# Two cross-attentions in one kernel: four exponential buffers, the keys ahead of the value products' sum, and a unit's normalisation at the end of ScalarE's and GpSimd's order

## The reference, cut to what is computed

```
x = x + tanh(g_xattn[0]) * xattn0(layernorm(x), ctx)      # 8 heads of 64
x = x + tanh(g_ffn[0])   * expert_choice(layernorm(x))    # sinkhorn, 16 experts
x = x + tanh(g_xattn[1]) * xattn1(layernorm(x), ctx)      # 16 heads of 64
x = x + tanh(g_ffn[1])   * top2_experts(layernorm(x))     # 8 experts

def xattn(x, context, Wq, Wk, Wv, Wo, bo):
    q, k, v = heads(x @ Wq), heads(context @ Wk), heads(context @ Wv)
    attn = softmax(q k^T * 64**-0.5)
    return merge(attn v) @ Wo + bo
```

## Time and profile before

| | |
|---|---|
| time, three runs | 2080.51, 2082.16, 2084.51 us; median 2082.16 |
| profiled execution | 2078.9 us, its span 2077.2 us |
| PE busy | 1849.3 us, 89% of the span |
| DVE, ACT, POOL busy | 77%, 76%, 31% |
| first attention | from about 30 to 383 us |
| second attention | from about 1360 to 1950 us |
| granted TensorE clock, mean | 0.973 |
| DMA transposes (L534) | 192, 3.0 us to landing |

### The profile page before, as it was taken

One profiled execution on the slowest core, in us unless ns is written; L12 is line 12 of the kernel. 1 busy time (PEld: TensorE's weight loads), 2 busy tenths in 40 slices (PEclk: granted clock), 3 DMA queues, 4 the chain that ended last, 5 costly groups with the idle time before them and its releaser, 6 DMA issues. The chain is left out here.

```text
span 2077.2 us, 73737 instructions
## 1 busy us (share of the span) xinstructions
PE 1849.3 (89%) x29130; PEld 1340.8 (65%) x29130; DVE 1599.2 (77%) x3619; ACT 1578.8 (76%) x2771; POOL 652.4 (31%) x893
## 2 busy tenths in 40 slices
PE   4898888784899999999999999968888889999698
PEld 3677777642466666666666667745666667777487
DVE  3778777797788888888888887767888887777654
ACT  3777778473798989898989898747777778887543
POOL 3677777502000000000000000035555555455465
PEclk9999999897799999999999999979999999999899
DMA  7433334275000000000000000046555553333233
GB/s 176 96 83 82 84 84 87 70 270 208 11 12 14 14 14 12 14 12 14 12 14 12 14 9 2 2 116 137 128 128 128 128 128 64 63 60 61 53 108 116
DMA packets 304575, 147.44 MB, mean 71 GB/s; under 512 B 235472, under 2 KB 289536, under 8 KB 304000
## 3 DMA queue, kind: packets, MB, share of 16 engines
q1 hardware_dynamic: 303824, 144.75, 28.1%
q10 hardware_dynamic: 560, 0.08, 0.0%
HBM read 55.45 MB, written 30.54 MB: 41 GB/s over the span
## 5 line engine op out<-in xcount | busy, mean ns | idle before, releaser
L1640 DVE TENSOR_TENSOR h<-g,h 128x1024 f16<-128x1024 f32 x256 | 313.3, 1224 | 140.9 <-ACT h L1585 140.9
L232 PEld LDWEIGHTS psE<-ew,h 128*128 128x128 f16 x6144 | 349.9, 98 | 54.6 <-issue 35.6
L232 PE MATMUL psE<-ew,h 128*128 128x128 f16 x6144 | 363.7, 219 | 11.9 <-DVE eo L1650 5.2
L232 PE MATMUL psH<-xg,ew 128*128 128x512 f16 x1536 | 356.1, 382 | 0.0
L1580 ACT ACTIVATE g<-psH,eb1T 128x512 f32<-128x512 f32 x512 | 330.4, 680 | 29.5 <-PE psH L232 23.0
L580 PE MATMUL psV<-Bw,cT 96*64 96x512 f16 x2304 | 319.7, 380 | 31.1 <-DVE vB L786 31.1
L755 POOL TENSOR_TENSOR E<-E,rden 128x512 f32<-128x512 f32 x192 | 200.1, 1042 | 257.0 <-DVE rden L795 257.0
L1585 ACT ACTIVATE h<-g 128x1024 f16<-128x1024 f32 x256 | 270.6, 1057 | 8.1
L1708 POOL MEMSET rbias<- 64x384 f32 x1 | 0.4, 411 | 855.6 <-POOLq L133 855.6
L660 PE MATMUL psS<-u,xTa 128*64 128x256 f32 x1536 | 209.2, 391 | 59.8 <-ACT u L718 54.5
L746 POOL TENSOR_TENSOR Ph<-E,Ph 128x512 f16<-128x512 f32 x192 | 222.4, 1159 | 120.8 <-ACT Ph L703 120.8
(11 more groups left out here) (256 smaller groups left out, 2774.3 us busy)
## 6 DMA issues: line engine op xcount, KB each, us to landing
keys_ahead<-ust SPq DMA_DIRECT2D x40, 512.0 KB, 4.8
u<-keys_ahead SPq DMA_DIRECT2D x40, 512.0 KB, 3.5
rawe<-in_L_ffn_w_dram SPq DMA_DIRECT2D x32, 256.0 KB, 2.8
wb<-rw SPq DMA_DIRECT2D x64, 128.0 KB, 2.0
rows<-places SPq DMA_DIRECT2D x110, 64.0 KB, 2.6
out_dram<-x SPq DMA_DIRECT2D x7, 512.0 KB, 3.2
context_T<-cT SPq DMA_DIRECT2D x64, 48.0 KB, 2.3
PT<-Ph SPq DMA_TRANSPOSE x192, 3.0
```

The costliest lines, as they stand in the source:

```text
L232: last = e.matmul(to, a, b, start=start and n == 0, stop=stop and n == 2, **flags)
L1640: e.tensor_tensor(h[:, 1 - par, 1, 2 * q:2 * q + 2, :], g32[:, 2 * q:2 * q + 2, :], h[:, 1 - par, 0, 2 * q:2 * q + 2, :], ALU.subtract)\
```

## The change

The exponential tile E gets four buffers in place of two, indexed by j mod 4, and the subtraction of j waits for the remainder of j-4. On PE the keys of j are issued right behind value product b (and the tokens' transpose), and PV of j-4 behind the keys. On ACT the copy Ph of j-2 goes from the middle to behind u of j; in the first attention xTa is thereby directly behind vB a. On POOL the multiply of j-1 and behind it the Ph remainder of j-2 go to the end, behind the bias and the expert weights. Nothing is added or left out.

```diff
-            E = sb(c, "E", [P, 2, 8, N], F32)
+            E = sb(c, "E", [P, 4, 8, N], F32)
...
+                    self.four = self.j.mod(4)
...
                         if a3.on:
                             values(a3, 1, "b")
+                        if first:
+                            tokens()
+                        if a.on:
...
+                            if not a.loaded:
+                                keys(a, 0)
+                                keys(a, 1)
                         if a4.on:
                             wait(e, s[f"pt{a4.par}"], ring_of(a4.j, 2, a4.par), 16)
...
                             last.then_inc(s["PV"], 1)
-                        if first:
-                            tokens()
-                        if a.on:
...
-                            if not a.loaded:
-                                keys(a, 0)
-                                keys(a, 1)
                         if a2.on:
                             values(a2, 0, "a", ready)
...
-                        if not first:
-                            tokens()
-                        if a2.on:
-                            wait(e, s["mul"], a2.j)
-                            wait(e, s[f"pt{a2.par}"], ring_of(a2.j, 2, a2.par) - 1, 16)
-                            e.activation(Ph[:, a2.par, 0].rearrange("p k t -> p (k t)"),
-                                         E[:, a2.par].rearrange("p h l -> p (h l)"), ACT.Copy)\
-                             .then_inc(s["phi"], 1)
-                        if first:
-                            tokens()
+                        tokens()
                         if a3.on:
                             value_hi(a3, 1, "b")
...
                                              psU[:, b, :], ACT.Copy).then_inc(s[f"uc{b}"], 1)
+                        if a2.on:
+                            wait(e, s["mul"], a2.j)
+                            wait(e, s[f"pt{a2.par}"], ring_of(a2.j, 2, a2.par) - 1, 16)
+                            e.activation(Ph[:, a2.par, 0].rearrange("p k t -> p (k t)"),
+                                         E[:, a2.four].rearrange("p h l -> p (h l)"), ACT.Copy)\
+                             .then_inc(s["phi"], 1)
...
+                        if a1.on:
+                            wait(e, s["rden"], a1.j)
+                            e.tensor_tensor(E[:, a1.four], E[:, a1.four],
+                                            rden[:, a1.par, :].unsqueeze(2).broadcast_to([P, 8, N]), ALU.mult)\
+                             .then_inc(s["mul"], 1)
+                        if a2.on:
+                            wait(e, s["phi"], a2.j)
+                            e.tensor_tensor(Ph[:, a2.par, 1].rearrange("p k t -> p (k t)"),
+                                            E[:, a2.four].rearrange("p h l -> p (h l)"),
+                                            Ph[:, a2.par, 0].rearrange("p k t -> p (k t)"), ALU.subtract)\
+                             .then_inc(s["plo"], 1)
...
-                            wait(e, s["plo"], a.j - 2)
-                            e.tensor_tensor(E[:, a.par], psS[:], top[:].unsqueeze(2).broadcast_to([P, 8, N]),
+                            wait(e, s["plo"], a.j - 4)
+                            e.tensor_tensor(E[:, a.four], psS[:], top[:].unsqueeze(2).broadcast_to([P, 8, N]),
```

More of the change, by code:

```diff
@@ L614, in body @@
                             values(a3, 1, "b")
+                        if first:
+                            tokens()
+                        if a.on:
+                            if a.opens:
+                                if first:
+                                    wait(e, s["ct"], a.t)
+                                else:
+                                    wait(e, s[f"ctx{a.ring}"], ring(a.t, a.ring), 16)
+                            if not a.loaded:
+                                keys(a, 0)
+                                keys(a, 1)
                         if a4.on:
@@ L628, in body @@
                             last.then_inc(s["PV"], 1)
-                        if first:
-                            tokens()
-                        if a.on:
-                            if a.opens:
-                                if first:
-                                    wait(e, s["ct"], a.t)
-                                else:
-                                    wait(e, s[f"ctx{a.ring}"], ring(a.t, a.ring), 16)
-                            if not a.loaded:
-                                keys(a, 0)
-                                keys(a, 1)
                         if a2.on:
@@ L711, in body @@
                             wait(e, s["sub"], a1.j)
-                            e.activation(E[:, a1.par], E[:, a1.par], ACT.Exp, bias=zero_col[:], scale=DH ** -0.5)\
+                            e.activation(E[:, a1.four], E[:, a1.four], ACT.Exp, bias=zero_col[:], scale=DH ** -0.5)\
                              .then_inc(s["exp"], 1)
@@ L743, in body @@
                              .then_inc(s["clo"], 1)
-                        if a2.on:
-                            wait(e, s["phi"], a2.j)
-                            e.tensor_tensor(Ph[:, a2.par, 1].rearrange("p k t -> p (k t)"),
-                                            E[:, a2.par].rearrange("p h l -> p (h l)"),
-                                            Ph[:, a2.par, 0].rearrange("p k t -> p (k t)"), ALU.subtract)\
-                             .then_inc(s["plo"], 1)
                         if a.opens:
@@ L752, in body @@
                             e.tensor_tensor(tile_of(a.t, x), tile_of(a.t, x), bo_rep[:], ALU.add).then_inc(s["bo"], 1)
-                        if a1.on:
-                            wait(e, s["rden"], a1.j)
-                            e.tensor_tensor(E[:, a1.par], E[:, a1.par],
-                                            rden[:, a1.par, :].unsqueeze(2).broadcast_to([P, 8, N]), ALU.mult)\
-                             .then_inc(s["mul"], 1)
                         if first and a.on:
@@ L792, in body @@
                             wait(e, s["mul"], a1.j - 2)
-                            e.tensor_reduce(den[:, a1.par, :], E[:, a1.par], AX.X, ALU.add).then_inc(s["den"], 1)
+                            e.tensor_reduce(den[:, a1.par, :], E[:, a1.four], AX.X, ALU.add).then_inc(s["den"], 1)
                             wait(e, s["den"], a1.j)
```

## The result

| | before | changed |
|---|---|---|
| median (9 runs each) | 2082.59 us | 2077.4 us (2070.53 to 2079.36) |
| ratio, 95% interval | 1 | 0.9966 [0.9954, 0.9979] |
| profiled execution, span | 2078.9, 2077.2 | 2073.0, 2071.3 |

A forecast was written before the change was run, and what follows sets the result against it. Taken as bound by where PE waits, in loops closing once per unit. Terms 0 (first attention), -8.4 (keys every unit), -13.2 (keys ahead), +1 (ends) sum to -20.6: 2058.3 from the profiled 2078.9, 2061.5 as median; range 2051 to 2075.

The forecast's parts named there:

- Keys every unit: Second attention, keys made each unit: a loop of 4.55 us per unit, pairs from 9.45 to 9.10, 8.4 us gained.
- Keys ahead: Second attention, odd units' keys ready made: pairs from 8.60 to 8.27 us, 40 pairs gaining 13.2 us (8 to 16).
- First attention: 60 units: PE's 0.54 us wait exchanged for another, 311.0 against 310.6 us; booked as nothing, range -3 to +12.
- The loop through L811: First attention: PV, DVE's addition (L813 before), den, vB remainder, value product, tokens, keys close a loop of 4.95 us.
- runs at PE's pace: Rival, first attention: if a counted step of the loop overlaps, 60 units gain 0.54 each; -32, time 2029; chance 0.05.
- Units 5 to 15: Second attention, five of the pairs with keys ahead: forecast to gain 1.6 us.
- Part 2: Normalisation at GpSimd's end: late remainder delays SP's keys load, odd scores 0.9 us late; pair 8.27, 13.2 us gained.
- a miss of some tenths: Second attention, keys ahead: transpose lands at 9.7 to 10.3, read at about 9.8; lateness falls into the keys' wait.
- The ends: End of each attention: last remainder follows a multiply and another remainder, 0.5 us later, twice, +1 us.
- the keys' load would push the pair beyond the old 8.60: Rival, keys ahead: load landing at L = 14.0 makes pairs 9.28, time about 2102; chance 0.06.
- DVE would be held by GpSimd in the normalisations: Rival, first attention: 18 stages each held 1.0 us by a GpSimd remainder; +18, time 2079.5; chance 0.04.

The follow-up runs named there:

- e4: The changed kernel with GpSimd's Ph remainder ahead of the bias and the multiply again in the second attention; 2067.46 us, ratio 0.9922.
- e10: The changed kernel with SP issuing the load of the ready made keys ahead of the odd unit's DMA transpose; 2069.65 us, ratio 0.9935.
- e1: The changed kernel with PV back ahead of the tokens' transpose and the keys, in the first attention alone; 2071.14 us, ratio 0.9942.
- e2: The changed kernel with DVE's addition of psY to x moved behind the next step's vB remainder in the first attention; 2040.17 us, ratio 0.9780.
- e9: The kernel before with DVE's addition of psY to x moved behind the next vB remainder in the first attention; 2083.87 us, ratio 0.9998.
- e3: The changed kernel with SP issuing the last stage's twelve weight loads at step 90 of the second attention, not step 8; 2076.93 us, ratio 0.9967.

## Why the prediction was wrong

**Keys every unit: right.** 8.4 forecast, 9.4 measured. The loop scores, maximum, subtraction, exponential, u has 4.46 to 4.6 where I had 4.55.

**Keys ahead, steady: right.** Pairs of 8.31 against 8.27, 9.9 us for 32 pairs against 10.5, and by the mechanism named: the load behind the late transpose (e4 and e10 both remove it, and both come out at PE's 8.19).

**First attention: mechanism right, size short.** The loop through L811 exists, as e1, e2 and e9 show. I had 4.95 and it is 5.01: L811 starts 0.99 after PV's start where I summed 0.87 and 0.06 (its hand over is 0.15, from 323.85 to 324.00). Every fourth unit, at the end of an unrolled loop, is 0.23 longer, so that units 46 to 62 average 5.06. Of the 2.9 us by which 313.9 lies over my 311.0, 1.4 are in the four steps from unit 4 (24.4 where I had 23.0). The first of these takes 7.32 and the others 5.68; from 62 to 66 us the granted clock is 0.57, where the kernel before had 1.00, and no term of the sum was for that. 0.6 are in the next 32 steps, 1.0 in the last 23. All this is inside the "-3 to +12" that I kept. But the rival "runs at PE's pace" was weighed as something that might happen by itself; what the rows offered was a kernel that makes it happen.

**Units 5 to 15: the step that failed.** Part 2 says of the transpose "a miss of some tenths, which falls into the wait for the keys". That was worked out for the steady pair and carried to all 40. I listed what stands behind the remainder on SP and not what stands ahead of the transpose: at step 8 that is twelve loads for the last stage. In the steady pairs before, a transpose had landed 3.7 us (even units) and 4.5 us (odd) before PV read it (medians); now it is 1.6 and 0.2, so at step 8 nothing is left to absorb a late one. The same loads that cost the kernel before 3.0 us (46.1 for five pairs of 8.62), or 4.9 in e9's profile, cost 9.8 (51.3 for five of 8.31). This took 6.8 us of the 20.6 between the two profiled executions, 4.9 if e9's is taken for the kernel before. Where those loads are issued later, units 5 to 15 take 43.1 (e3), so they are the cause of the gap; 1.75 of it came by the clock, which fell in PE's wait and for which the forecast had no term. The place could be seen before: the load of the keys that was issued at 1412.72 landed 6.3 us later and PE waited 2.84 for it, but the landings of 3.2 to 3.8 in the earlier trace rows leave it out. The whole trace has up to 8.5.

**The ends: under-sized.** I had 0.5 for each. The last L811 of the first attention comes 2.2 us later after the last unit than before; the second attention's 0.9 later, and 1.2 more passed after it, in code that was not touched and that varies (126.7 to 129.3 in these profiles). The 2.2 is not all the change's order: at a granted clock of 1.00 this end takes 10.3 us in the kernel before and 11.6 in e4, whose first attention is the changed kernel's, and 12.5 in the changed kernel's own profile, at 0.93. That the 1.3 between the first two is the remainder waiting for the multiply is argued and not shown.

**What is left.** 20.6 less 3.3 (first attention), 6.8 (gap), 3.3 (ends) and 1.2 (between the attentions), plus 0.4 (steady pairs, 9.9 + 9.4 against 10.5 + 8.4), gives 6.4; 0.5 more is missing in the first units (0.6 of about 1.1). That is the 5.9 between the profiled executions; the medians are 5.2 apart.

**The rivals.** That the keys' load would push the pair beyond the old 8.60 didn't happen; it sets the pair, at 8.31. That DVE would be held by GpSimd in the normalisations didn't either: units 8 to 39, with two of the three parts, average 5.37 where 5.15 plus 6.2/31 gives 5.35. Before, twelve of the normalisations' operations overlapped one of GpSimd's in the first attention and five of them took 0.27 to 0.36; now four do and none takes over 0.18. So the rule of the Trainium skill (SBUF — State Buffer, "Who interferes with whom"), that a VectorE instruction with two SBUF inputs and a GpSimd instruction that reads SBUF get in each other's way, cost nothing here.

## What to carry to other kernels

When work is moved so as to fill a wait, list for every engine the instructions that stand behind the moved one's reader: here one addition a unit, free before, turned a gain of 32 us in the first attention into a 3 us loss there, and moving it gave 2040 us. A step with no slack in the steady loop must be followed through the places where the loop isn't steady, above all through queues that also carry somebody else's transfers. And an order that puts an operation behind one that waits (GpSimd's remainder behind a multiply that waits for rden) delays all that hangs on it, on other queues too. Read the granted clock of each stretch that is compared, in both profiles, before a difference is put down to an order.

## What the runs showed of the hardware

PE to DVE took 0.15 us after PV's end, as the profile models it, in the changed kernel (323.85 to 324.00), where the forecast had 0.06 from the other direction. A DMA transpose on SP takes 1.23 us to issue, and 3.82 when it stands behind ten small loads and two of 512 KB; from issue to landing it took 3.1 us in the middle and 6.4 at worst (the changed kernel, SP's line of the transpose):

```profile
DMA to landing us min/median/max: 3.0/3.1/6.4
```

TensorE's granted clock fell from 1.00 to 0.50 in a wait of PE's of 5.71 us in the changed kernel and in one of 2.01 in e9, and not in one of 2.84 in the kernel before. Scores that take 1.08 us took 1.92 and 1.97 at 0.50.

The profiles of kernels with the same code between the attentions differ by up to 4.4 us there, nearly as much as the whole change is worth; only the unit starts inside the attentions (equal to 0.1 us a pair from run to run, where no DMA is waited for) could carry the account.
